# Cross attentions 2 and 3: where the last four tiles' probabilities are turned, and in which order the last weighings run

## The reference

```
q = norm(x) @ wq;  k = y @ wk;  v = y @ wv                   # y: the context, 64 tokens a sequence
a = softmax(q @ k.T * d ** -0.5)                              # 16 heads, 64 columns each
o = concat over heads of (a @ v)                              # [tokens, 512] in 2, [tokens, 256] in 3
# cross attention 2 goes on with its tail:
x_out = x0 + o @ li1_w + li1_b
h = gelu(norm(x_out) @ li2_w + li2_b);  y = x_out + h @ li3_w + li3_b
```

## Time and profile before

| | us |
|---|---|
| median of 3 runs | 1981.5 (1980.46 to 1983.92) |
| the profiled execution, its own time | 1976.22 |
| its span in the trace | 1974.5 |
| TensorE busy in the span | 1789.1 (91%) |
| VectorE busy | 1284.4 (65%) |
| ScalarE busy | 1035.4 (52%) |
| GpSimd busy | 693.3 (35%) |
| granted TensorE clock, mean | 0.968 of 2.4 GHz |

### The profile page before, as it was taken

The page is one execution under the profiler, slowest core; times in us unless marked ns, Lnnn a source line. Parts: engine busy times, 40 slices in busy tenths (PEclk is TensorE's granted clock), DMA queues, the critical chain, the costliest instruction groups (busy, mean ns, idle before and its releaser), DMA issues. The chain is left out here.

```text
span 1974.5 us, 32334 instructions
## 1 busy us (share of the span) xinstructions
PE 1789.1 (91%) x11430; PEld 1164.3 (59%) x11430; DVE 1284.4 (65%) x2762; ACT 1035.4 (52%) x2194; POOL 693.3 (35%) x995
## 2 busy tenths in 40 slices
PE   6989999999899999998899989999999999872697
PEld 3445555555566666766567765557767555551597
DVE  5579999999734476232789963259999353868311
ACT  3489999999622354221677741147776211642232
POOL 0023333333334435142455641125555210450343
PEclk9999999999999998999999999999999999977799
DMA  3451111110000020020100002020000000037495
GB/s 122 136 165 45 44 45 44 44 44 2 1 1 1 0 60 1 1 65 8 39 6 5 4 7 70 0 59 3 7 7 7 6 0 12 6 114 186 117 329 157
DMA packets 102959, 97.23 MB, mean 49 GB/s; under 512 B 37056, under 2 KB 86544, under 8 KB 102672
## 3 DMA queue, kind: packets, MB, share of 16 engines
q1 hardware_dynamic: 99216, 90.84, 15.3%
q0 software_dynamic: 3584, 4.33, 1.1%
HBM read 78.23 MB, written 14.81 MB: 47 GB/s over the span
## 5 line engine op out<-in xcount | busy, mean ns | idle before, releaser
L613 DVE TENSOR_REDUCE negmax<-sps 128x1 f32<-128x1024 f32 x256 | 309.2, 1219 | 17.1 <-PE sps L535 12.6
L657 ACT ACTIVATE prob<-sps,negmax 128x1024 f32<-128x1024 f32 x256 | 285.7, 1117 | 23.2 <-DVE negmax L613 18.7
L1943 POOL TENSOR_TENSOR la_pr_x3kblk<-la_pr_x3kblk,la_ri 128x512 f32<-128x512 f32 x128 | 158.5, 1268 | 152.3 <-DVE la_ri L2042 152.3
L703 POOL TENSOR_TENSOR probT<-probT,after 128x128 f32<-128x128 f32 x256 | 116.9, 457 | 237.6 <-DVE probT L621 211.7
L2271 ACT ACTIVATE la_pr_x3kblk<-la_pr_x3kblk,la_nx 128x256 f32<-128x256 f32 x256 | 126.4, 495 | 100.9 <-DVE la_nx L2083 100.9
L535 PE MATMUL sps<-ks,qs 128*128 128x512 f16 x512 | 168.8, 381 | 7.8 <-PEq L42 3.1
L2493 PE MATMUL la_bs<-lf_zT,lfw 128*128 128x512 f32 x352 | 153.4, 594 | 0.0
L551 PE MATMUL tps<-ident,prob 128*128 128x128 f32 x704 | 125.3, 282 | 22.7 <-DVE probT L621 20.3
L551 PEld LDWEIGHTS tps<-ident,prob 128*128 128x128 f32 x704 | 79.7, 141 | 89.3 <-issue 43.7
L1953 POOL TENSOR_TENSOR la_qs<-la_qn,ores 128x256 f32<-128x256 f32 x128 | 97.1, 789 | 77.7 <-DVE la_qn L2099 77.7
L1585 PE MATMUL tx_s<-t_zT,tw 128*128 128x512 f32 x256 | 113.8, 593 | 1.1 <-ACT t_zT L1452 1.1
(11 more groups left out here) (378 smaller groups left out, 3870.4 us busy)
## 6 DMA issues: line engine op xcount, KB each, us to landing
w1e<-in_fc_T SPq DMA_DIRECT2D x16, 1024.0 KB, 5.7
w2e<-in_fc_T SPq DMA_DIRECT2D x16, 1024.0 KB, 8.8
qs<-q_parts SPq DMA_DIRECT2D x128, 64.0 KB, 1.9
ks<-k_parts SPq DMA_DIRECT2D x128, 64.0 KB, 1.9
q_parts<-parts SPq DMA_DIRECT2D x8, 512.0 KB, 3.7
k_parts<-parts SPq DMA_DIRECT2D x8, 512.0 KB, 3.6
tw<-in_L_xattn_a_li_w SPq DMA_DIRECT2D x4, 1024.0 KB, 8.2
lfw<-in_L_ffn_w SPq DMA_DIRECT2D x6, 640.0 KB
```

Of the source, the lines that this page charges most:

```text
L613: dve.tensor_reduce(negmax[:, n % 4:n % 4 + 1], slots[n % NS][:], X, ALU.max, negate=True).then_inc(s.max_done, 1)
L657: act.activation(prob[:, n % 3, :], slots[n % NS][:], ACT.Exp, bias=negmax[:, n % 4:n % 4 + 1], accum_out=rowsum[:, tile % 2, n % QUAD:n % ...
L703: pool.tensor_tensor(blk, blk, after[:], ALU.mult).then_inc(s.masked, 1)
L1943: ins = pool.tensor_tensor(prob[:, h:h + 2, :], prob[:, h:h + 2, :], rinv[:, h:h + 2].unsqueeze(2).to_broadcast([P, 2, 2 * P]), ALU.mult)
```

## The change

Both attentions get a function `turned(t, half)`, which names the bank for a turned half. Up to tile 11 it is the old one. From tile 12 on the halves go to: the old bank, `sps[0]` first half; `sps[1]` first, `sps[1]` second; `sps[0]` second, the old bank; `sps[1]` first, `sps[1]` second. Transposes and copies use it. The waits of the last turnings become `prob_ready` of tile 14 or 15 (the score pair is read), or the copy of an earlier half that had the same bank. TensorE's loop ends one turn after the last scores, and the rest is written out. In attention 2 the turning of the norm comes behind the last half, VectorE's norm behind the loop (behind tile 15's shares), and ScalarE's scale and shift behind the last copy. The weighings and everything before tile 12 keep their code.

```diff
+                def turned(t, half):
+                    tail = ((pbank[:], sps[0][:, 0:512]), (sps[1][:, 0:512], sps[1][:, 512:1024]),
+                            (sps[0][:, 512:1024], pbank[:]), (sps[1][:, 0:512], sps[1][:, 512:1024]))
+                    return pbank[:] if t < NT - 4 else tail[t - NT + 4][half]
...
@@ VectorE, attention 2
                             if it == NT - 3:
                                 first_sum(s2, 0)
-                            if it == NT - 2:
-                                normed_sum(s2, 0)
+                        normed_sum(s2, 0)
                         hidden_input(s2, 1)
...
@@ ScalarE, both: the copy of a half
-                            act.copy(pT[:, t % 2, half * 512:(half + 1) * 512], pbank[:]).then_inc(s.pT_done, 1)
+                            act.copy(pT[:, t % 2, half * 512:(half + 1) * 512], turned(t, half)).then_inc(s.pT_done, 1)
...
@@ ScalarE, attention 2
+                            if live(it - 1):
+                                evacuate(it - 1, 1)
                             if it == NT:
                                 normed(s2, 0)
-                            if live(it - 1):
-                                evacuate(it - 1, 1)
...
@@ TensorE, turn_sum of attention 2
-                                pe.wait_ge(s.prob_ready, NT)
+                                pe.wait_ge(s.pT_done, 2 * (NT - 2) + 1)
...
@@ TensorE, turn_probs (in 3 the same, with its own first case)
-                            else:
+                            elif t < NT - 4 or (t, half) == (NT - 4, 0):
                                 pe.wait_ge(s.pT_done, 2 * t + half)
+                            elif t == NT - 4:
+                                pe.wait_ge(s.prob_ready, NT - 1)
+                            elif t == NT - 3:
+                                pe.wait_ge(s.prob_ready, NT)
+                            elif (t, half) == (NT - 2, 1):
+                                pe.wait_ge(s.pT_done, 2 * (NT - 4) + 1)
+                            elif t == NT - 1:
+                                pe.wait_ge(s.pT_done, 2 * (NT - 3) + half + 1)
                             for r in range(NP2 // 2):
                                 at = (half * NP2 // 2 + r) * P
-                                mm = pe.transpose(pbank[:, r * P:(r + 1) * P], prob[:, t % NPB, at:at + P], ident[:])
+                                mm = pe.transpose(turned(t, half)[:, r * P:(r + 1) * P], prob[:, t % NPB, at:at + P], ident[:])
...
@@ TensorE, the loop (attention 2; in 3 without turn_sum)
-                        for it in range(NT):
+                        for it in range(NT - 3):
...
+                        for t in (NT - 4, NT - 3):
+                            turn_probs(t, 0)
+                            turn_probs(t, 1)
+                            weigh(t)
+                        turn_probs(NT - 2, 0)
+                        turn_probs(NT - 2, 1)
                         turn_probs(NT - 1, 0)
+                        weigh(NT - 2)
+                        turn_probs(NT - 1, 1)
                         turn_sum(s2, 0)
-                        turn_probs(NT - 1, 1)
                         weigh(NT - 1)
```

More of the change, by code:

```diff
@@ L769, in cross_attention @@
                 HALF, HH = P // 2, HQ // 2
+                def turned(t, half):
+                    tail = ((tps[:], sps[0][:, 0:512]), (sps[1][:, 0:512], sps[1][:, 512:1024]),
+                            (sps[0][:, 512:1024], tps[:]), (sps[1][:, 0:512], sps[1][:, 512:1024]))
+                    return tps[:] if t < NT - 4 else tail[t - NT + 4][half]
                 def spot(r):
@@ L855, in evacuate @@
                                 act.wait_ge(s.pv_done, t - 1)
-                            act.copy(pT[:, t % 2, half * 512:(half + 1) * 512], tps[:]).then_inc(s.pT_done, 1)
+                            act.copy(pT[:, t % 2, half * 512:(half + 1) * 512], turned(t, half)).then_inc(s.pT_done, 1)
                         def exponent(t):
@@ L905, in turn_probs @@
                                 pe.wait_ge(s.qT_done, QPAIR)
-                            if t > 0 or half == 1:
+                            if 0 < t < NT - 4 or (t, half) in ((0, 1), (NT - 4, 0)):
                                 pe.wait_ge(s.pT_done, 2 * t + half)
+                            elif t == NT - 4:
[6 more added lines that the diff above has]
+                                pe.wait_ge(s.pT_done, 2 * (NT - 3) + half + 1)
                             for r in range(NP2 // 2):
                                 at = (half * NP2 // 2 + r) * P
-                                mm = pe.transpose(tps[:, r * P:(r + 1) * P], prob[:, t % NPB, at:at + P], ident[:])
+                                mm = pe.transpose(turned(t, half)[:, r * P:(r + 1) * P], prob[:, t % NPB, at:at + P], ident[:])
                             mm.then_inc(s.p_turned, 1)
@@ L958, in score @@
                             mm.then_inc(s.scores, 1)
-                        for it in range(START, NT + 1):
+                        for it in range(START, NT - 3):
                             if live(it - 1):
@@ L972, in _ @@
                                 weigh(it - 1)
+                        for t in (NT - 4, NT - 3):
[4 more added lines that the diff above has]
+                        turn_probs(NT - 2, 1)
+                        turn_probs(NT - 1, 0)
+                        weigh(NT - 2)
+                        turn_probs(NT - 1, 1)
+                        weigh(NT - 1)
                 release(s)
```

## The result

The changed kernel takes 1970.87 us (median of 4 runs, 1968.83 to 1972.5), the kernel before 1982.71 us beside it (4 runs, 1980.46 to 1984.37): 11.8 us less, ratio 0.9950 with a 95% interval of 0.9934 to 0.9967. The forecast was 1972.0 us, 9.5 us less. The profiled execution has a span of 1970.7 us and a time of 1972.5 us.

A forecast was written before the change was run, and what follows sets the result against it. In both attention tails TensorE and ScalarE take turns with one bank, with TensorE's clock low. Gains of 4.0 + 4.0 + 1.5 = 9.5 us off 1981.5 give 1972.0 us, range 1968.5 to 1978.0.

The forecast's parts named there:

- (a): Attentions 2 and 3, tiles 12 to 15: own banks for halves end the copy wait; 4.0 us each, orders included.
- rise inside the unbroken stretch: Both tails: the clock comes back 3.3 to 5.3 us into unbroken TensorE work; the forecast case, chance 0.60.
- my rival of a high clock: Clock hardly falls in the tails or is back at once: 14.2 us gained, 1967.3 us; chance 0.10.
- (b): Both tails: tile 15's first half ahead of weighing 14 fills TensorE during a copy; cost nothing, bound 0.3 us.
- (c): Attention 2: norm turned behind tile 15's second half, affine copies last; takes 1.3 us of transposes off the path.
- (d): Attention 2: VectorE's norm behind tile 15's shares, which start 0.65 us earlier; norm hidden by 1 to 3 us.
- (e): Unedited router phase behind attention 3: first 48 matmuls gain from a risen clock; 0 to 2.1 us, taken as 1.5.
- Clock low in both tails: Rival: the clock stays low in both attentions' tails; only 4.3 us gained, 1977.2 us; chance 0.15.
- Gain hidden: Rival: banks weren't the hold or ScalarE's order keeps it; one tail gains 1.3 to 3.0 us, about 1979.5; chance 0.11.
- Slower: Rival: clock not back before attention 2's hidden projections, which then run slower; 1985.5 us; chance 0.04.

The follow-up runs named there:

- run 8: The changed kernel itself, unedited, timed again beside the kernel before: 1969.00 against 1981.83 us, ratio 0.9938.
- run 3: The changed kernel's banks and waits, but all orders of the kernel before: 1969.87 us, ratio 0.9955 to the kernel before.
- run 7: The changed kernel with VectorE's norm back ahead of tile 15's shares in attention 2: 1969.45 us, ratio 0.9942 to the kernel before.
- run 9: The changed kernel with tile 14's weighing ahead of tile 15's first half in both attentions: 1970.14 us, ratio 0.9962 to the kernel before.
- run 10: The changed kernel with attention 2's norm turned ahead of tile 15's second half, affine copies ahead of the last copy: 1969.37 us, ratio 0.9946 to before.
- run 1: The changed kernel with attention 3 put back to the old code, so attention 2 only: 1975.07 us, ratio 0.9971 to the kernel before.
- run 2: The changed kernel with attention 2 and its tail put back to the old code: 1972.83 us, ratio 0.9963 to the kernel before.
- run 11: The changed kernel with filler transposes in both tails and attention 2's tile 13 first half turned before tile 12's weighing: 1965.56 us, ratio 0.9932 to before.

## Why the prediction was right, step by step

**(a) Banks.** The mechanism held. No turning waits for the other half's copy; tiles 12 and 13 gained nothing (tile 13's weighing 9.85 us behind tile 11's, 9.47 in run 8, 9.49 before), since ScalarE's order sets them. I took 4.0 us for each attention; 4.4 and 4.3 were measured in the first trace, 5.5 and 5.7 in run 8. From weighing 13 to the hidden projection I had 8.5 to 8.8 us and it was 7.84, as the clock was already up at 785.88; from weighing 13 to the last output copy's end 6.7 to 7.3, and it was 6.65.

**The clock.** The rise inside the unbroken stretch came as said in attention 3: work unbroken from 1749.70, rise at about 1753. The other four traces with the new banks that lost it there (runs 3, 7, 9, 10) had it back at the same place, 11.1 us behind tile 11's weighing; the two with the old code, before and run 1, had it low until 24.8 us behind it.

In attention 2 it went another way: back once before that stretch, at about 783.8, by the weighing and eight transposes from 780.31 to 784.04, down again after the 1.84 us wait, and up at about 790.6, which is the rise inside the unbroken stretch that I had forecast. The traces of runs 1, 7 and 10 do the same; runs 3, 8 and 9 have the first rise alone. That first rise is not the change's doing: run 2's old code has it too (19.31 us). Two things I had taken as fixed are not: that the old code stays low for 13.7 us, and that work of 3.0 us without a gap does not bring the clock back (in run 2 it did, 779.93 to 782.92). So attention 2's term came out near its 4.0 us with some luck, while attention 3's came as forecast. Runs 2 and 8 went through attention 3 as in my rival of a high clock. It was a mixture by execution, and the time landed between the forecast's and that case's.

**(b), (c) Orders.** Counted inside (a); by themselves worth 2.8 us in the marks (run 3), of which weighing 14's place is about 1.7 and the norm's turning 1.1. I had left both inside (a) without a figure of their own, and named for (b) only a cost, at nothing; its gain is the larger of the two.

**(d) The norm behind the shares.** 3.17 us beside GpSimd's share (I had 2.88 from before), ending at 789.49, two us ahead of its turning at 791.50. Hidden, and needless too: run 7 without the step has the same 17.74 us. The Trainium skill's rule for the shared port pair (SBUF — State Buffer, "SBUF: two separate sides") gives the pair to whichever engine starts first, for its whole instruction. This trace agrees: VectorE's second and third instruction started behind a share of GpSimd's and ended 0.15 us behind it. The four took 3.17 us against 1.38 alone, while GpSimd's two shares took 2.11 (2.04 alone).

**(e) The router phase.** The term that was mis-sized: 1.5 us taken, 2.6 measured in the first trace (1.3 left at the first top-8 in runs 2 and 8). Two errors of mine. The pace that I took from a later row of 16 overstates an unbroken run of 48, which needs 10.60 us and not 11.16; the 5.3 us at the low clock that I had named myself point to 2.65 us. And VectorE, full as it was from 1768 on, started earlier by as much, so it gave nothing away: in the first trace the first top-8 moved by the same 2.6 us. What took some of it back in other executions was the clock, not VectorE.

**The rivals.** Clock low in both tails: in none of the ten traces with the new banks in both does it stay down to the end of a tail. Gain hidden: fell with runs 1 and 2. Slower: in no trace is the clock down at the first hidden projection.

## What to carry to other kernels

When one engine waits for another by turns, price the wait twice: what it takes itself, and what it does to TensorE's clock. Here the second was the larger, 10.4 us against 4.4 in the traces, and could be measured by itself with filler transposes whose results nobody reads. Compare two traces by distances between marks around the edit, since chance elsewhere (4.5 us here) is as large as what one attention gained, and take more than one trace of the kernel before too (22.08 and 19.31 us for the same code); and follow a shortened stretch into the next phase, where the clock may fall in the gap that it left.

## What the runs showed that I had not expected

The same kernel has several speeds in one stretch: attention 2's tail of the changed kernel 17.69 and 16.54 us, attention 3's 15.13 and 13.73, with nothing else that I found different in the trace than where the low stretches lie. The kernel before, in 16 runs beside runs 9 to 11, has two clusters, seven runs from 1975.4 to 1977.4 and nine from 1980.6 to 1983.7 us; a median of few runs can sit in either. Run 2 has two as well, six runs from 1969.0 to 1970.8 us and six from 1974.8 to 1977.5, and its trace is of the second. And 14 extra transposes cost nothing where TensorE waits, but 8 behind the last weighing, ahead of a barrier, cost 0.6 us.
